# Another hand-over order for four streams of a two-layer decoder kernel

## The reference

```python
x = x + L0_attn(ln(x))         # 16 heads of 16, low-rank k and v, rotation
x = x + L0_xattn(ln(x), ctx)   # per token: 16 heads x 16 heads of 64
x = x + L0_ffn(ln(x))          # top half of the tokens by a router, gelu FFN 256-1024-256
x = x + L1_attn(ln(x))         # 16 heads, the 25 largest scores of a row are kept
x = x + L1_xattn(ln(x), ctx)   # 16 heads, keys beyond a length are masked
x = x + L1_ffn(ln(x))          # ternary 256x256 linear layer
```

## Time and profile before

| | us |
|---|---|
| median of 3 runs | 6784.98 (6783.06 to 6803.64) |
| profiled execution | 6756.82 |
| its span | 6755.0 |
| 29 passes of the loop | 461.83 to 6285.67 in the span |
| passes h, t, c / t, c / c | 183.5 / 181.4 / 104.4 |
| PE busy | 5896.7, 87% of the span |
| DVE, ACT, POOL busy | 4510.2, 4012.6, 1507.3 |

### The profile page before, as it was taken

The page is one execution under the profiler, slowest core; times in us unless marked ns, Lnnn a source line. Parts: engine busy times, 40 slices in busy tenths (PEclk is TensorE's granted clock), DMA queues, the critical chain, the costliest instruction groups (busy, mean ns, idle before and its releaser), DMA issues. The chain is left out here.

```text
span 6755.0 us, 109667 instructions
## 1 busy us (share of the span) xinstructions
PE 5896.7 (87%) x37509; PEld 3877.2 (57%) x37762; DVE 4510.2 (67%) x16186; ACT 4012.6 (59%) x9761; POOL 1507.3 (22%) x2564
## 2 busy tenths in 40 slices
PE   6888988988988988898888898888898898898876
PEld 3565565565565565565565565566556556556542
DVE  1366766666777666776676676666776666677653
ACT  2465666565666665666656566656566655566632
POOL 0122222222222222222222222222222222222211
PEclk7789989899999899999999899999998999999965
DMA  2000000000000000000000000000000000000000
GB/s 79 4 6 6 4 8 6 8 8 6 4 8 7 6 8 6 4 8 8 6 8 6 6 6 8 6 8 7 7 4 8 6 8 8 6 4 8 4 2 5
DMA packets 29456, 54.18 MB, mean 8 GB/s; under 512 B 8145, under 2 KB 9810, under 8 KB 27986
## 3 DMA queue, kind: packets, MB, share of 16 engines
q1 hardware_dynamic: 28770, 45.73, 2.1%
HBM read 37.33 MB, written 8.39 MB: 7 GB/s over the span
## 5 line engine op out<-in xcount | busy, mean ns | idle before, releaser
L914 POOL TENSOR_TENSOR t_pr<-t_pr,sc 128x512 f32<-128x512 f32 x512 | 649.6, 1269 | 1495.9 <-ACT t_pr L839 1495.9
L350 DVE TENSOR_REDUCE m_nm<-bankM 128x2 f32<-128x512 f32 x1024 | 657.0, 683 | 347.9 <-PE bankM L340 344.0
L887 DVE MATCH_REPLACE8 wk<-m,wk 128x256 f32<-128x256 f32 x2048 | 821.0, 408 | 0.0
L340 PE MATMUL bankM<-m_kT,m_q 32*128 32x256 f32 x4096 | 698.5, 466 | 75.4 <-DVE m_nm L350 74.3
L883 DVE MAX8 m<-wk 128x8 f32<-128x256 f32 x2048 | 759.2, 412 | 0.0
L651 ACT ACTIVATE xk_area<-bankH,xb 64x256 f32<-64x256 f32 x1024 | 480.7, 469 | 460.4 <-PE bankH L546 438.1
L394 PE MATMUL bankM<-m_q,m_kT 32*128 32x512 f32 x2048 | 627.9, 691 | 0.0
L883 DVE MAX8 m<-sc 128x8 f32<-128x256 f32 x1024 | 380.0, 412 | 327.5 <-ACT sc L830 290.1
L340 PEld LDWEIGHTS bankM<-m_kT,m_q 32*128 32x128 f32 x4096 | 411.3, 216 | 312.4 <-DVE m_nm L350 133.6
L845 ACT ACTIVATE t_pr<-t_pr,t_nm 128x256 f32<-128x256 f32 x1024 | 463.9, 504 | 182.5 <-POOL t_pr L914 180.5
L408 ACT ACTIVATE m_pT<-bankM,keymask 128x512 f32<-128x512 f32 x512 | 323.7, 683 | 247.4 <-PE bankM L394 247.4
(11 more groups left out here) (207 smaller groups left out, 12011.2 us busy)
## 6 DMA issues: line engine op xcount, KB each, us to landing
xin<-x_in SPq DMA_DIRECT2D x32, 256.0 KB, 2.6
ctxA<-ctx_in SPq DMA_DIRECT2D x32, 256.0 KB, 2.6
ctxB<-ctx_in SPq DMA_DIRECT2D x32, 256.0 KB, 3.5
out<-x SPq DMA_DIRECT2D x32, 256.0 KB, 2.0
w<-w_w SPq DMA_DIRECT2D x2, 1024.0 KB
xwq<-w_xwq SPq DMA_DIRECT2D x1, 1024.0 KB
xwk<-w_xwk SPq DMA_DIRECT2D x1, 1024.0 KB
xwv<-w_xwv SPq DMA_DIRECT2D x1, 1024.0 KB
```

The costliest lines, as they stand in the source:

```text
L340: last = nc.tensor.matmul(bank[x][:, j * S:(j + 1) * S], b["q2"][r:r + 32, e, j, t * P:(t + 1) * P], b["kT"][r:r + 32, e, :], start=not ma ...
L350: nc.vector.tensor_reduce(b["nm"][:, i % 2, 2 * (i // 2) + x, :], banks[u % 3][:].rearrange("p (j s) -> p j s", j=2), AX.X, ALU.max, negat ...
L887: m = nc.vector.match_replace(out=wk[:, k, t, :], in_to_replace=take, in_values=src[:, t, :], imm_value=-BIG)
L914: nc.gpsimd.tensor_tensor(sp_[:, u % 2], taken[:, u % 2], sc[:, u % 3], ALU.mult).then_inc(g["sp_mul"], 1)
```

## The change

Only the table `ORDER` is replaced. Every stream has as many letters as before on every engine, so the same instructions are issued, each stream's own steps in the same order; only the interleaving differs, in the loop's passes and in the shorter ones. The new table comes from a plan in which the duration of a matmul depends on how much of the array it uses.

```diff
     "pe": runs("""
-        t h c m h2 c t h2 t h t h t h2 c h2 t h2 c h2 t h c h2 t c t h c t h c h c t c h2 c t h c t2 h2 c h c3 t c2 h2 c2 h c2 t c h2 t c3 t
-        h c2 h2 c t h c3 h t h t h t h3 c t h m c t m2 t h m t h m t m2 t m2 h m t h m h m t h6 m t h2 m h t m4 t m2 t m3 t m5 t m t m t m t m t"""),
+        t h c m h2 c t h c h t c t h c t h c t h2 c h3 c h2 c t h c h2 c h t c t h t h c4 t h c2 h2 c2 t c2 h t c h t h2 c3 t h3 c2 t h2 t c
+        h t c2 h2 c t h2 t h t h c t h c h2 t h m t m2 t m t h m h m t m2 t h m t h m h m t h5 m h3 m t h m4 t m2 t m3 t m3 t m2 t m t m t m
+        t m"""),
     "act": runs("""
-        t h c m h4 c2 t h3 t7 h4 t h t h3 c h2 t h t h2 t h c h t3 h3 t h3 t h t h t2 h3 t h4 t3 h4 t h t h4 t h t2 h c3 h2 t c2 h3 t c2 t2
-        h2 c2 h2 t c2 h2 t c3 h t h4 c2 t2 h c2 t h c t h2 t h t h c h t h t h t h t h t h t h c t4 m t m4 t h t2 h t h t4 h2 t h t m t2 h t
-        m2 t3 m2 t m2 t m2 t2 m2 t m3 t2 m2 t m2 t m t m t"""),
+        t h c m h4 c2 t c h3 t7 c h2 t2 h2 t h4 t h3 t h3 t2 h2 t h2 t h3 t h t3 h2 c3 h t h4 c2 h t3 h c2 h3 t c2 h3 t c2 h3 t c2 h t2 c h3
+        t h2 t3 h c2 h2 t h3 t c2 h t h c h t2 h3 c t h3 t3 h3 t h t h t h c t2 h2 t h t4 m t m4 t3 h t h t3 h t2 h2 t h t2 m t h m2 t3 m2 t
+        m2 t m2 t2 m2 t m3 t2 m t m t m2 t m t m"""),
     "dve": runs("""
-        t h c m t h t h c t h c3 t12 c2 t2 c2 t h c2 t h c2 t h c2 h t c2 t c2 h2 t c2 t2 h2 t3 h t4 h2 t4 h2 t2 h2 t c3 t h t2 c t c t c t
-        c t m t m t m t2 h t c h t h2 m2 t m2 h2 m2 h2 m2 h3 m2 t m2 t2 m2 t m2 t3 h2 t2 h t6 m3 t3 m t"""),
+        t h c m t h t h c t c2 h c t c2 t2 c2 t2 c2 t2 c2 t c2 t2 c2 t2 c2 t2 c2 h t h t5 h t h2 t2 h2 t2 h2 t4 h2 t4 h2 c3 t2 h2 t c t c h
+        t c t c t m t m t c m t5 h t h t h2 m4 t m2 h2 m2 h5 m2 t3 m2 t m2 t m2 t10 h3 t3 m3 t m"""),
     "pool": runs("""
-        t h c m t h t h t h c2 t10 h t2 h c t3 h t h t h t3 h t3 h t h t2 c2 t3 c t m2 t2 h3 t6 m t10"""),
+        t h c m t h t2 h c h c t8 c t3 h2 t3 h t2 h t3 h t h t3 h t3 h c3 t m t m t4 h3 t6 m t10"""),
```

More of the change, by code:

```diff
@@ L60 @@
     "pe": runs("""
-        t h c m h2 c t h2 t h t h t h2 c h2 t h2 c h2 t h c h2 t c t h c t h c h c t c h2 c t h c t2 h2 c h c3 t c2 h2 c2 h c2 t c h2 t c3 t
-        h c2 h2 c t h c3 h t h t h t h3 c t h m c t m2 t h m t h m2 t m2 h m t h m h m t h6 m t h2 m h t m4 t m2 t m3 t m5 t m t m t m t m t"""),
+        t h c m h2 c t h c h t c t h c t h c t h2 c h3 c h2 c t h c h2 c h t c t h t h c4 t h c2 h2 c2 t c2 h t c h t h2 c3 t h3 c2 t h2 t c
+        h t c2 h2 c t h2 t h t h c t h c h2 t h m t m2 t m t h m h m t m2 t h m t h m h m t h5 m h3 m t h m4 t m2 t m3 t m3 t m2 t m t m t m
+        t m"""),
     "act": runs("""
-        t h c m h4 c2 t h3 t7 h4 t h t h3 c h2 t h t h2 t h c h t3 h3 t h3 t h t h t2 h3 t h4 t3 h4 t h t h4 t h t2 h c3 h2 t c2 h3 t c2 t2
-        h2 c2 h2 t c2 h2 t c3 h t h4 c2 t2 h c2 t h c t h2 t h t h c h t h t h t h t h t h t h c t4 m t m4 t h t2 h t h t4 h2 t h t m t2 h t
-        m2 t3 m2 t m2 t m2 t2 m2 t m3 t2 m2 t m2 t m t m t"""),
+        t h c m h4 c2 t c h3 t7 c h2 t2 h2 t h4 t h3 t h3 t2 h2 t h2 t h3 t h t3 h2 c3 h t h4 c2 h t3 h c2 h3 t c2 h3 t c2 h3 t c2 h t2 c h3
+        t h2 t3 h c2 h2 t h3 t c2 h t h c h t2 h3 c t h3 t3 h3 t h t h t h c t2 h2 t h t4 m t m4 t3 h t h t3 h t2 h2 t h t2 m t h m2 t3 m2 t
+        m2 t m2 t2 m2 t m3 t2 m t m t m2 t m t m"""),
     "dve": runs("""
-        t h c m t h t h c t h c3 t12 c2 t2 c2 t h c2 t h c2 t h c2 h t c2 t c2 h2 t c2 t2 h2 t3 h t4 h2 t4 h2 t2 h2 t c3 t h t2 c t c t c t
-        c t m t m t m t2 h t c h t h2 m2 t m2 h2 m2 h2 m2 h3 m2 t m2 t2 m2 t m2 t3 h2 t2 h t6 m3 t3 m t"""),
+        t h c m t h t h c t c2 h c t c2 t2 c2 t2 c2 t2 c2 t c2 t2 c2 t2 c2 t2 c2 h t h t5 h t h2 t2 h2 t2 h2 t4 h2 t4 h2 c3 t2 h2 t c t c h
+        t c t c t m t m t c m t5 h t h t h2 m4 t m2 h2 m2 h5 m2 t3 m2 t m2 t m2 t10 h3 t3 m3 t m"""),
     "pool": runs("""
-        t h c m t h t h t h c2 t10 h t2 h c t3 h t h t h t3 h t3 h t h t2 c2 t3 c t m2 t2 h3 t6 m t10"""),
+        t h c m t h t2 h c h c t8 c t3 h2 t3 h t2 h t3 h t h t3 h t3 h c3 t m t m t4 h3 t6 m t10"""),
 }
```

## The result

The changed kernel takes 6832.23 us (median of 9 runs, 6813.83 to 6862.98) against 6783.06 for the kernel before (9 runs, 6742.09 to 6814.2). The ratio is 1.0079, with a 95% interval of 1.0049 to 1.0109: slower by 49 us, where 33 were forecast. The profiled execution of after took 6832.23 us, 75.4 more than that of before.

What follows compares the result with a forecast made beforehand. PE was taken to bound the kernel, with only its idle time and clock able to change. The terms summed to +1.4 us a pass, +41 over 29 passes, less 8 in short passes: +33, about 6818 us, range 6705 to 6890.

Steps and rivals of the forecast that it cites:

- its own criteria: Wrong if y to ln5 is well under 8 us, loop idle no higher, or mean clock 0.93 moves over 0.01.
- Term 1: c's scores, placed among h's projections: no waits there, but 0.9 us ahead of the first sT; gain 1.3 a pass.
- Term 2: c's sT stage: 1.35 us wait stays, ACT nearly ties with PE; 3.7 us of waits, loss 1.8 a pass.
- Term 3: c's out1, out2 and y: two steps of h cover the 0.69 us ahead of y; gain 0.4 us a pass.
- Term 4: c's y to ln5: less work covers 8.27 us; idle 4.1 against 2.4, loss 1.7, plus 0.4 behind ln5.
- Term 5: m's first scores: two waits partly covered by h's ln2 and sps, 1.4 us for 2.2; gain 0.8 a pass.
- The short passes: Passes t, c and h, t, c: five of c's scores now ahead of the 5.29 us wait for t; gain 8 us.
- Rival 1: Clock gains, ending long half-clock stretches in c's sT stage: about 6716 us; chance 0.33, shared with lesser gains.
- Rival 2: Clock loses: waits of Term 4 let it fall in most passes, +43 to +87 us, 6861 to 6905; chance 0.13.

Runs made afterwards that it cites:

- two experiments that undo it, in whole and in part: Against the filled kernel: t s5, h o6, tr7, o7 ahead of c's ln5 with ACT's copy moved, 6702.23 us; only t s5 and h o6, 6620.96 us.
- kernel with the old first half: Old tables up to m's keys and values, the new ones from there: 6698.79 us, ratio 0.9896 to the kernel before.
- filled kernel: New kernel plus three full-array matmuls in each of two waits of c (ahead of first sT, between first and second): 6592.67 us, ratio 0.9748.
- narrow fillers: The filled kernel with its added matmuls on 32 rows of the array instead of 128: 6662.98 us, ratio 0.9815 to the kernel before.
- the fillers in out2's wait: Kernel with the old first half and three full-array matmuls between c's first two sT, plus two between out1 and out2: 6533.32 us, 6520.31 without the two.

## Why the prediction was right, and where it was wrong

The forecast said slower, by 33 us, within 6705 to 6890; measured was slower by 49. The sign holds, and most waits did what they were laid out to do. That the size holds too is luck. The sum gave +41 us of waits in the loop and the waits gave 16; 58 of the 74 us lost there are something the sum had at zero; and the two profiled executions, for which it was made, differ by 75 us, not 33. By its own criteria it is wrong in one: the loop's share of the clock moved from 0.93 to 0.91.

**Term 1 (c's scores), -1.3: measured -1.0.** No wait over 0.3 us among them, as laid out. The one ahead of the first sT is 0.94 us, as forecast (0.9). The 2.2 us of before were read a little high: the 0.53 of the earlier trace rows has one matmul for two weight loads and is 0.30 up to the load, so 1.9 became 0.9.

**Term 2 (sT stage), +1.8: measured +1.0.** The waits are 1.35 + 0.85 + 0.50 = 2.7 us, for a forecast 3.7, against 1.35 + 0.19 + 0.20 = 1.7 before (again up to the weight load where a record is missing). The largest new one is for `xpt` of h rather than for c's exponentials.

**Term 3 (out, y), -0.4: measured -0.5.** 0.23 + 1.14 us stay, the 0.69 are gone.

**Term 4 (y to ln5), +1.7 and +0.4: measured +1.1 and +0.7 where the clock is full.** tr5 waits 2.23 us (forecast 2). In the fastest pass the stretch is 7.85 us, 3.56 of it idle, for a forecast 8.27 and 4.1, and 2.4 before. In the typical pass it is 8.15 with only 2.8 idle, because the clock falls within it and the slower matmuls fill the gap. ln5 was to wait about 2 us for L291; it waits 0.69 there and not at all in the typical pass. Behind ln5, o7 waits 0.69 for ACT. The two experiments that undo it, in whole and in part, did not win the cost back.

**Term 5 (m's scores), -0.8: measured -0.1, and wrong in what it counted.** The waits for DVE's maxima are 0.64 + 0.88 = 1.5 us for 2.2 before (forecast 1.4), but two new ones, 0.20 and 0.33, take most of that back. Yet the stage is where the change gains: its largest wait fell from 1.39 to 0.88 us and the half clock from 14.5 to 4.1 us a pass. The kernel with the old first half shows that gain alone, 1% of the time.

**The short passes, -8: measured 0.** h, t, c took 7.7 us more (191.2 for 183.5) and t, c 8.0 less (173.3 for 181.4). The gain in t, c is the one laid out; that h, t, c would lose as much was not seen, and no experiment looked at it.

**The step that failed** is "PE's work stays at 177 us a pass at full clock", with the clock left to the rivals. Summed, the terms gave an idle time of +1.4 us a pass, and it was +0.5; the busy time, at 0, was +2.0. Rival 1 expected the 72-row steps of `h` in the sT stage to end its half clock; they didn't, and ran at half clock themselves (L580's 259 us became 318). Rival 2 had the right mechanism, waits that let the clock fall in most passes, and its price was near (43 to 87 us for the 58 of busy time measured), but it put the fall at term 4. There it rose by 3.8 us a pass; the sT stage gave 14.9. The row to have drawn this from was there: the half clock followed a 1.35 us wait with narrow matmuls behind it, and term 1 set a second wait just ahead of the first. Its price of 0.9 us of idle time was right; what stands next to it was not looked at.

The Trainium skill's page "TensorE: Matmul & The Clock Gate", Part 4 (PE-mode transpose), has the full clock not engage for transposes. By that rule y to ln5 would be cold in every pass. The window of the filled kernel over that stretch has a clock of 1.00 with 3.5 us idle in 7.85 and transposes as four of its seven steps of work, so here they did not end it at once.

**What stays open.** Why the clock falls at a given wait in one pass and not in the next; why 16 passes of the new kernel lock at 204.8 us; whether the clock would fall at these waits with wide matmuls behind them; why narrow fillers hold the clock in most passes and not in all; why m's half clock varies among kernels with the same second half (3.4 to 7.8 us a pass, and 13.7 with term 4 undone); and why the fillers in out2's wait gave nothing.

## What to carry to other kernels

When an order is changed on an engine with two clocks, compare the granted clock of every stage before and after, as well as the waits: the same instructions can cost more at the same idle time. A wait of about a microsecond with matmuls on few rows behind it was the place here, and full-array work of no other use put into it can pay for itself. Count the matmuls of a step against its weight loads before a wait ahead of it is priced: a missing record reads as idle time. Before a step is moved to cover a wait, find the chain that ends the wait, on the other engine: within that chain the move gains nothing, and an early step may be early for an engine behind it.

## What the runs showed of the hardware that was not expected

- Adding 3.1 us of matmuls to a pass made it 7.5 us shorter (203.4 to 195.9).
- The half clock lasts while PE is busy for nearly all of the time: 23.64 of 23.89 us in the sT stage of the kernel with narrow fillers, as 20.18 of 20.40 in the earlier trace rows:

```profile
1494.78:1518.67 23.89, 23.64 (x105) 10.69 (x108) 11.97 (x48) 14.64 (x47) 4.72 (x6) 0.50 0.00 0
```

- Waits of 0.94 and 1.35 us, 4 us apart, were enough for 23.9 us at half clock in 23 of 29 passes; behind the 1.35 alone it was 3.4 us in 23 of 29 passes and 13.7 or 20.5 in six.
- The same sequence of instructions can settle into a repeating state that is 5% slower than its own best pass: 204.8 against 195.0 us.
